# A three-layer decoder kernel: 32-key mask slabs, setup scaling on ACT, early window products shared with DVE, new delays

## The reference, cut to what matters

```python
x = x + local_attn(layernorm(x))      # each token sees the 7 tokens around it, with bq, bk, bv, bo
x = x + cross_attn(layernorm(x), ctx) # 120 context rows, with bq, bk, bv, bo
y = layernorm(x)
y = y + causal_attn(rmsnorm(y, n1_w)) # keys later than the query are masked out, no biases
h = rmsnorm(y, n2_w)
w = sum of the two largest of softmax(h @ gate_w.T), over (that sum + 1e-9)
out = x + y + w * (silu(h @ up_w.T) @ down_w.T)     # 1024 hidden channels
```

## Time and profile before

| | us |
|---|---|
| median of three runs | 3643.12 |
| lowest and highest | 3640.56, 3643.16 |
| the profiled execution | 3645.45 |
| its span | 3643.7 |
| busy: PE, DVE | 3531.3, 2772.1 |
| busy: POOL, ACT | 2506.0, 1720.3 |
| PE busy in the first 217 us | 148.5 |
| PE busy from 400 to 3460 us | 3039.0 of 3060 |
| mean granted clock of PE | 0.988 |

### The profile page before, as it was taken

One profiled execution on the slowest core, in us unless ns is written; L12 is line 12 of the kernel. 1 busy time (PEld: TensorE's weight loads), 2 busy tenths in 40 slices (PEclk: granted clock), 3 DMA queues, 4 the chain that ended last, 5 costly groups with the idle time before them and its releaser, 6 DMA issues.

```text
span 3643.7 us, 97036 instructions
## 1 busy us (share of the span) xinstructions
PE 3531.3 (97%) x38792; PEld 2886.4 (79%) x38792; DVE 2772.1 (76%) x6256; ACT 1720.3 (47%) x4049; POOL 2506.0 (69%) x3156
## 2 busy tenths in 40 slices
PE   6799999999999999999999999999999999999998
PEld 5578888888888888888888888888888888888876
DVE  5677787787787787787787787777777777877863
ACT  2344545445545545544445445545545444445443
POOL 5767767767767667667677677677677677677642
PEclk8899999999999999999999999999999999999999
DMA  5111111111111111121121121121121111111100
GB/s 175 47 49 62 56 66 60 58 66 59 59 67 52 63 70 48 66 71 45 67 73 45 66 73 45 66 74 45 66 73 45 66 67 51 66 62 56 66 8 10
DMA packets 87098, 221.54 MB, mean 61 GB/s; under 512 B 8262, under 2 KB 53634, under 8 KB 70274
## 3 DMA queue, kind: packets, MB, share of 16 engines
q1 hardware_dynamic: 86658, 215.34, 16.9%
HBM read 164.92 MB, written 50.39 MB: 59 GB/s over the span
## 4 chain that ended last, share of the span: by engine, by line
PE 91%; DVE 4%; ACT 2%; DMA 1%; issue 1%; POOL 1%; SPq 0%; DVEq 0%; POOLq 0%; ACTq 0%
PE ps L858 13%; PE ps L867 12%; PE ps L720 11%; PE ps L698 9%; PE ps L837 9%; PE ps L754 8%; PE ps L809 8%; PE ps L786 6%; PE ps L726 4%; PE ps L678 3%; PE ps L778 3%; PE ps L747 2%; PE ps L847 2%; DVE held L1347 1%; DVE nmax_pair L1284 1%; ACT rest L1000 1%
## 5 line engine op out<-in xcount | busy, mean ns | idle before, releaser
L1115 POOL TENSOR_TENSOR chunks<-v_windows,xT 128x560 f32<-128x560 f32 (+1 forms) x384 | 869.9, 2285 | 256.7 <-DVE xT L1259 153.8
L1284 DVE TENSOR_REDUCE nmax_pair<-ps 128x4 f32<-128x480 f32 (+2 forms) x1280 | 775.4, 668 | 176.7 <-PE ps L754 176.7
L1110 POOL TENSOR_TENSOR chunks<-rest,k_windows 128x512 f32<-128x512 f32 (+1 forms) x384 | 552.2, 1453 | 448.0 <-DVE xT L1238 230.9
L967 ACT ACTIVATE prob<-ps 128x256 f32<-128x256 f32 (+2 forms) x1536 | 670.2, 548 | 332.2 <-PE ps L786 332.2
L858 PE MATMUL ps<-xT,w_up 128*128 128x256 f32 x2048 | 486.3, 386 | 0.0
L867 PE MATMUL ps<-w_down,held 128*128 128x256 f32 x2048 | 458.9, 382 | 1.8 <-DVE held L1347 1.6
L867 PEld LDWEIGHTS ps<-w_down,held 128*128 128x128 f32 x2048 | 383.9, 190 | 72.2 <-issue 20.4
L858 PEld LDWEIGHTS ps<-xT,w_up 128*128 128x128 f32 x2048 | 377.8, 192 | 45.5 <-issue 0.9
L925 ACT COPY xT<-ps 128x512 f32<-128x512 f32 x256 | 149.8, 585 | 511.6 <-PE ps L678 511.6
L1238 DVE TENSOR_REDUCE xT<-chunks 128x32 f32<-128x512 f32 (+1 forms) x384 | 293.7, 765 | 119.6 <-POOL chunks L1110 119.5
L1127 POOL TENSOR_SCALAR_AFFINE_SELECT prob<-prob 128x512 f32<-128x512 f32 x512 | 319.4, 654 | 87.0 <-ACT prob L967 86.9
(11 more groups left out here) (143 smaller groups left out, 6161.1 us busy)
## 6 DMA issues: line engine op xcount, KB each, us to landing
k_windows<-passed_on SPq DMA_DIRECT2D x64, 1024.0 KB, 4.6
v_windows<-passed_on SPq DMA_DIRECT2D x64, 1024.0 KB, 5.1
x<-in_x SPq DMA_DIRECT2D x64, 256.0 KB, 3.0
passed_on<-rest SPq DMA_DIRECT2D x64, 256.0 KB, 2.0
passed_on<-held SPq DMA_DIRECT2D x64, 256.0 KB, 2.0
out<-x SPq DMA_DIRECT2D x64, 256.0 KB, 2.2
y<-in_ctx SPq DMA_DIRECT2D x64, 120.0 KB, 2.9
w_up<-in_up SPq DMA_DIRECT2D x1, 1024.0 KB, 8.9
```

What stands on the lines that cost most here:

```text
L967: last = nc.scalar.activation(prob_pair(seq, L, m)[0:keys, :, r, col:col + qs], of_pair, ACT.Exp, scale=SCALE)
L1110: last = nc.gpsimd.tensor_tensor(chunk_of(c).rearrange("p (j d) -> p j d", d=D), q_row, window("k", (b + first) * D, (D, n), (1, D)), ALU. ...
L1115: last = nc.gpsimd.tensor_tensor(chunk_of(c).rearrange("p (h i j) -> p h i j", i=HD, j=WINDOW), window("v", b * D + first * HD, (HD, n), ( ...
L1284: nc.vector.tensor_reduce(nmax[s][:, tb, heads], src, AX_X, ALU.max, negate=True).then_inc(emptied[b], 1)
```

## The change

1. The mask by slabs of 32 keys: slab s covers only keys 32 s to 32 s + 31. That is enough, since the weights of the slab (`pick_rows`) now hold, beside the query's own row, a one in the slab's last row for every query before the slab, and that row of the mask is all -1e30. Still 16 mask matmuls for each fill; 128 keys by 4 or by 2 head pairs in all where it was 320.
2. Even products of the first 3 sequences (`EARLY`) go to DVE, odd ones stay on POOL. A fetch of windows then waits for both.
3. The scaling of weights goes from DVE to ACT, in three parts (`causal`, `up`, `down`); `down` now waits for its own.
4. The biases of cross attention are loaded in the order needed; DVE keeps two small instructions.
5. New durations in the planner, a new `STAY` (1500 for 210) and a new `DELAY` table.

```diff
-DIVIDE, REJOIN, CHANGE = 0.33, 0.2, 0.1
-STAY = 210.0
+DIVIDE, REJOIN, CHANGE = 0.4, 0.2, 0.2
+EARLY = 3
+STAY = 1500.0
...
-DELAY = {("gate", None, "PE"): 55, ("project", 2, "PE"): 2975, ("project_out", 1, "PE"): -85,
...
+DELAY = {("max", 2, "PE"): -15, ("project", 2, "PE"): 1785, ("project_rows", None, "PE"): 10,
...
-                a = part("window_times", (c,), "POOL", pool, ready + reduced[-2:-1],
...
+                if early and c % 2 == 0:
+                    a = part("window_times", (c,), "DVE", dve + 0.4, ready + reduced[-2:-1],
+                             [("chunks", ())] if c == 0 else [])
+                else:
+                    a = part("window_times", (c,), "POOL", pool, ready + reduced[-2:-1],
...
-                                sp.dma_start(bias_heads[what[-1]][:], bass.AP(src.tensor, src.offset, [
-                                    [0, P // HD], [H, HD], [1, H]])).then_inc(loaded[n], 16)
+                                    sp.dma_start(bias_whole[what[-1]][:], bass.AP(src.tensor, src.offset, [
+                                        [2, 4], [1, 2], [H, HD], [H // 2, 2]])).then_inc(loaded[n], 16)
...
+                            if before[0] < EARLY:
+                                sp.wait_ge(reduced[plan.lane[before[0]]],
+                                           reached["reduced", "window_reduce", before[0], (c - 1,)])
...
-                                    later = mask_rows[rows, slab, 32 * slab:P].unsqueeze(1)
-                                    nc.tensor.matmul(of_heads[:, :, tb * P + 32 * slab:(tb + 1) * P],
-                                                     pick_rows[rows, slab, :],
-                                                     later.to_broadcast([32, count, P - 32 * slab]),
+                                    first = tb * P + SLOT * slab
+                                    nc.tensor.matmul(of_heads[:, :, first:first + SLOT], pick_rows[rows, slab, :],
+                                                     mask_rows[rows, :].unsqueeze(1).to_broadcast([32, count, SLOT]),
...
+                        if what == "causal":
+                            for k in range(2):
+                                last = nc.scalar.activation(W["causal_v"][:, k], W["causal_v"][:, k], ACT.Identity,
+                                                            scale=scale1[:, k:k + 1])
+                        elif what == "up":
+                            for w in (w_up, w_gate):
+                                for k in range(2):
+                                    last = nc.scalar.activation(w[:, k], w[:, k], ACT.Identity,
+                                                                scale=scale2[:, k:k + 1])
+                        elif what == "down":
+                            last = nc.scalar.activation(w_down[:], w_down[:], ACT.Identity, scale=0.5)
...
+                            for e in range(2):
+                                last = nc.vector.tensor_scalar(bias_q[e][:], bias_whole["q"][:], half[:, e:e + 1],
+                                                               None, ALU.mult)
...
+                    elif name == "window_times":
+                        c, = args
+                        before = plan.before["chunks", seq, ()]
+                        if c:
+                            dve.wait_ge(reduced[s], reached["reduced", "window_reduce", seq, (c - 2,)])
...
+                        multiply_chunk(nc.vector, s, c).then_inc(multiplied_here[s], 1)
```

More of the change, by code:

```diff
@@ L69 @@
 Part = namedtuple("Part", "name args engine busy lag after takes gives")
-LAG = {"PE": 0.21, "ACT": 0.15, "DVE": 0.15, "POOL": 0.1}
+LAG = {"PE": 0.26, "ACT": 0.15, "DVE": 0.15, "POOL": 0.1}
 DMA_ISSUE = 0.42
@@ L155, in sequence_parts @@
         added = [part("norm", (layer,), "POOL", 1.37, [normed])] if layer < CAUSAL else []
-        turned = through("turn", (layer,), 0.4, "ACT", 0.49, [normed])
+        turned = through("turn", (layer,), 0.45, "ACT", 0.49, [normed])
         if layer == LOCAL:
@@ L205, in sequence_parts @@
                 held.append(a)
-                a = part(*step, "ACT", 2.3 if u < 2 else 2.6, [a] + first[1::2], (), [("quad", step)])
+                a = part(*step, "ACT", 2.0 if u < 2 else 2.25, [a] + first[1::2], (), [("quad", step)])
                 held.append(a)
@@ L213, in sequence_parts @@
                      [("prob", (layer, m)) for m in range(2)])
-            attended = part("normalise", (layer,), "DVE", 2.8, [a], (), halves)
+            attended = part("normalise", (layer,), "DVE", 2.84, [a], (), halves)
         if layer == LOCAL:
-            attended = through("turn_out", (), 0.4, "ACT", 0.57, [attended])
+            attended = through("turn_out", (), 0.5, "ACT", 0.57, [attended])
         done = through("project_out", (layer,), 1.63, "DVE", 0.6, [attended], also=added)
@@ L221, in sequence_parts @@
     added = part("norm", (3,), "POOL", 1.23, [done])
-    turned = through("turn", (3,), 0.4, "ACT", 0.49, [normed])
+    turned = through("turn", (3,), 0.45, "ACT", 0.49, [normed])
     gated = ("gate", (), "PE")
@@ L386, in __init__ @@
         for name, n, args in self.order["PE"]:
-            for kind, use in parts[at[name, args, "PE"]].takes:
+            for kind, use in of[n][at[name, args, "PE"]].takes:
                 if kind not in free:
@@ L510, in decoder @@
         loaded = [sem(f"loaded{n}") for n in range(len(LOADS))]
-        derived = {what: sem(f"derived_{what}") for what in ("pick", "bias", "scale", "cross", "causal")}
+        derived = {what: sem(f"derived_{what}") for what in ("pick", "bias", "cross", "causal", "up", "down")}
         filled = [sem(f"filled{b}") for b in range(BANKS)]
@@ L891, in _ @@
                         what, = args
[L892 to L894 removed]
+                        n = {"cross": 2, "causal": 3}.get(what, 4)
+                        once(act, known, f"weights{n}", loaded[n], 16 * len(LOADS[n]))
+                        for w in "qk" if n < 4 else "":
                             name = f"{what}_{w}"
```

212 lines of the change are left out of this document (109 added, 103 removed).

## The result

The changed kernel takes 3615.68 us, median of four runs (3613.7 to 3621.6), against 3642.01 for the kernel before in the same rounds: a ratio of 0.993, with a 95% interval from 0.9915 to 0.9945. That is 26 us less where 44.5 were forecast; 3598 was named, 3584 to 3619 was the range. The profiled execution took 3614.79 us, with a span of 3612.8.

A forecast was written before the change was run, and what follows sets the result against it. PE, busy in 97% of the span, was taken as the bound. Masks 38.5 us plus start 6 make 44.5 off the profiled 3645.45, so 3601; against the median, 3598 was named, with a range of 3584 to 3619.

The forecast's parts named there:

- rival (a): Mask matmuls on PE: narrow rounds cost a full one, masks save 26 us and the start 6: 3611 us; chance 0.12.
- What bounds the kernel, the masks: PE, busy in 97% of the span: shorter mask blocks save 0.61 us a sequence, 38.5 us counted in all.
- The line: Cost of a mask block on PE: 0.41 ns a column and 0.02 us beside it; at most 0.64 us a sequence saved.
- Whether the middle follows: Steady rounds: no other engine becomes late, some 0.8 us stay to spare at `turn`, so masks count in full.
- (c): Steady rounds: mask time becomes longer waits for DVE or ACT, only the start gains: 3637 us; chance 0.07.
- (d): Steady rounds: POOL's moments come late for `turn`, PE loses 1.4 us net a round: 3721 us; chance 0.05.
- The start: Chunks of sequence 0: left 9 us earlier through setup and shared products, 3 given back, so 6 us gained, from 0 to 14.
- Rival (b): Start: gains all 14 us of the chunks and 8 of the clock, with the masks: 3583 us; chance 0.08.
- Give back 3: Start: 3 of the 9 us lost to products of sequences 1 and 2 on DVE, some ahead of sequence 0's maxima.
- The end: nothing, 3 either way: PE's last three sequences: slightly other order with the same kinds of waits, no change, 3 us either way.

The follow-up runs named there:

- experiment 1: The kernel before with the narrow masks alone, all orders as before: 3607.3 us, ratio 0.9900.
- experiment 8: The kernel before with narrow masks and new setup (scaling on ACT, biases in order), products on POOL, old order: 3597.3 us, ratio 0.9871.
- experiment 4: The changed kernel with EARLY = 0, all products on POOL: 3606.4 us, ratio 0.9898.
- experiment 3: The changed kernel with the old DELAY values for sequences 62 and 63 alone: 3604.0 us, ratio 0.9892.
- experiment 5: The changed kernel with EARLY = 0 and the old DELAY values for sequences 62 and 63: 3600.4 us, ratio 0.9878.
- experiment 11: The changed kernel with EARLY = 0 and, from the `down` of sequence 57 on, every engine's list from the kernel before: 3595.3 us, ratio 0.9863.
- experiment 10: The kernel before with narrow masks and biases in order, the planner told the bias part takes 0.4 us on DVE, not 4.6: 3600.7 us, ratio 0.9882.

## Why the prediction was right, and where it was not

The time lies in the range, and faster was right. The sum was too hopeful by 18 us against the median, and by 14 between the profiled executions, which it was made of. Nearest to the measured time is the number of rival (a), 3611, whose mechanism the blocks rule out: a gain that was larger at the start and a loss at the end happen to add up to about that.

- **What bounds the kernel, the masks.** Right. Blocks of 0.22 and 0.11 us for 0.23 and 0.12 to 0.13; 57 rounds gave 35.1 us, 0.62 each, for a forecast of 0.61. Alone they are worth 38 us (experiment 1). In the new order they are worth less, 28.9 of the 35.1 us by the profile with the wide masks (3128.8 us for the 57 rounds), and the rest is the order, which the forecast put at nothing. The 3.7 us for the other six sequences aren't seen: the third `down` comes no earlier with the masks alone (327.8), and the old end took 180.9 us with wide masks and 175.1 to 181.1 with narrow ones. Rival (a), narrow rounds at a full one's cost, is out. (The line gives 0.62 us a sequence as the most that can be saved, not 0.64; nothing hangs on it.)
- **Whether the middle follows.** Right. The round is 54.33 us for a forecast of 54.4; rivals (c) and (d) are out.
- **The start.** The size is right and the reasons are half wrong. `turn_out` of sequence 0 came at 59.3 (near 59 forecast), the first `down` at 205.2 (209). Rival (b), 14 us of chunks and 8 of clock, is out: from 60 to 110 us the clock rose only from 0.62 to 0.67. At the third `down` the gain is 9.0 us for 6, or 7 with two sequences' masks; in two other executions with the same start it is 8.7 and 4.5. But the step that gave the chunks' 9 us to setup and products together was wrong: the setup alone takes 10.5 us off the chunks and 13.2 off the third `down` (experiment 8), and the products on DVE add 1.3 us to the chunks of sequence 0. The prediction compared DVE's new list with its own bounds, 24.5 to 35.7 us; it never asked what the chunks would take with the setup gone and POOL alone. From the earlier trace rows that is 39.1 - 6.8 - 4.7 = 27.6, less than the 30 forecast with sharing. "Give back 3" had the right place and was too small: with DVE products the third `down` is at 318.7, 319.0 and 323.2 us, without them at 314.9, 312.4 and 317.4, so they cost some 5 us there in the mean, about the spread of each three. It named products ahead of the maxima that POOL holds up; most of what the profile shows is POOL being late for the moments (experiment 4). The price of a product of probabilities and v, 0.86 and 0.73 us, was taken from additions and was too low by 0.5 and 0.4.
- **The end: nothing, 3 either way.** This is the step that failed: 13.2 us in the profiled execution, 11.6 when it ran again. It read "a slightly other order, with the same kinds of waits" off the list and did not price the swaps. The one of `project_out` 63 and `down` 62 could have been priced from the trace of before: `down` covers 3613.32 to 3620.23, and within it DVE, POOL and ACT make the norm that `turn` needs. ACT's norm is done at 3618.0, ahead of the end of `down`. Take `down` away from there, and its cover is gone. Experiments 3 and 5 put this at 12 and 6 us, and the whole new end against the old one at 11 (experiments 4 and 11, 190.6 and 179.2 us). In the five kernels with the new end 60th to 63rd `down` take 151.5 us in the mean, in the seven with the old one 148.6; so the rest of the new end may be worth some 3 us, which is within the scatter (144.7 to 150.7 in the old end alone).

## What to carry to other kernels

In a list that is fixed ahead, a swap in the steady round costs its wait once a round, but the last sequences have little other work to hide anything: read the last two of each chain part by part, and ask what covers the latency behind the last projection. Before work is shared between two engines, take off the waits that other edits remove and look at what is then left to share. A number in a planner that is out of date keeps a wait whose work is gone, and the wait then looks as if the edit had been worth nothing.

## What the runs showed of the hardware

The same list of instructions takes different times at the end, and the granted clock goes with it. This is the stretch from the 62nd to the 63rd `down` of two kernels with the same list there, experiment 8 first and then experiment 10, in windows:

```profile
3512.70:3566.50 53.80, 46.70 (x510) 36.64 (x507) 20.36 (x49) 20.27 (x53) 13.61 (x25) 0.87 0.02 6
```

```profile
3519.20:3568.20 49.00, 41.59 (x510) 33.01 (x507) 20.26 (x49) 20.01 (x53) 13.65 (x25) 0.97 0.02 7
```

53.8 us at a clock of 0.87 and 49.0 at 0.97, with the same 510 matmuls. PE idles for some 7 us in both. From 400 to 3460 us, where PE hardly idles, the clock is 1.00 before and after, and in every kernel at least 49 of the 57 rounds lie within 0.05 us of their median. From the 63rd to the last `down` the clock goes with the idle time without exception: in the nine kernels with `project_out` ahead of `down` PE idles for 2.2 to 2.3 us of 18 and the clock is 1.00, in the five executions without it PE idles for 6.8 us and the clock is 0.82 to 0.88. There the idle time cost more than itself, some 2.9 us in `turn`, `gate` and `up`. From the 60th to the last `down` the changed kernel idles for 9.4 us more than the kernel before (24.9 against 15.5) and lost 13.2; that the other 3.8 follow from the idle time isn't shown, since the stretch above scatters by 4.8 with the same idle time.
